# Two graph-attention layers on one core: the probabilities turned on VectorE and through DRAM, and the context taken transposed on column halves of the array

## The reference

```python
def layer(x, adj, Wq, bq, Wk, bk, Wv, bv, Wf, bf):      # 6 heads of 64
    h = relu(layernorm(x))
    q, k, v = heads(h @ Wq + bq), heads(h @ Wk + bk), heads(h @ Wv + bv)
    scores = einsum('bhqd,bhkd->bhqk', q, k) / 8
    probs  = softmax(scores + where(adj, 0, -9e15))
    ctx    = merge(einsum('bhqk,bhkd->bhqd', probs, v))
    return x + ctx @ Wf + bf
x = layer(x, adj, *weights_of_layer_0)
x = layer(x, adj, *weights_of_layer_1)
```

## Time and profile before

| | |
|---|---|
| median of three runs | 2083.96 us (2080.9 to 3268.01) |
| the profiled execution | 2084.19 us, span of its instructions 2081.6 us |
| TensorE matmul, weight load | busy 2023.3 us (97%), 1220.2 us (59%) |
| VectorE | 1757.7 us (84%) |
| ScalarE | 1268.3 us (61%) |
| GpSimd | 1335.0 us (64%) |
| DMA | 264.90 MB, 127 GB/s over the span |
| granted TensorE clock, mean | 0.992 of 2.4 GHz |

### The profile page before, as it was taken

How to read it: one execution, slowest core, us unless ns; L and a number is a source line. 1 busy time by engine, 2 the same in 40 slices (tenths; PEclk the granted TensorE clock), 3 DMA queues, 4 the chain that set the end, 5 groups by cost and what they waited for, 6 DMA issues and landing times.

```text
span 2081.6 us, 62061 instructions
## 1 busy us (share of the span) xinstructions
PE 2023.3 (97%) x18838; PEld 1220.2 (59%) x18838; DVE 1757.7 (84%) x6080; ACT 1268.3 (61%) x2249; POOL 1335.0 (64%) x1808
## 2 busy tenths in 40 slices
PE   4999999999999999999999999999999999999997
PEld 1556566566566556656665666666666666666664
DVE  6888888888888788888887888888888888888875
ACT  3566666666666566666665666666666666666653
POOL 3566666666666666666665666666666666666652
PEclk8999999999999999999999999999999999999998
DMA  6344444444444444444444444444444444444433
GB/s 192 98 113 120 131 127 123 129 135 135 136 122 125 121 135 135 134 115 130 132 137 127 129 119 133 131 135 136 127 119 133 131 136 136 129 117 117 114 98 99
DMA packets 443711, 264.90 MB, mean 127 GB/s; under 512 B 341986, under 2 KB 443364, under 8 KB 443364
## 3 DMA queue, kind: packets, MB, share of 16 engines
q1 hardware_dynamic: 443364, 260.76, 45.1%
HBM read 134.75 MB, written 125.83 MB: 125 GB/s over the span
## 4 chain that ended last, share of the span: by engine, by line
PE 37%; issue 26%; POOL 25%; DMA 4%; DVE 3%; SPq 3%; ACT 1%; POOLq 1%; DVEq 0%; ACTq 0%
PE ps_proj L497 7%; PE ps_proj L499 7%; PE ps_proj L498 7%; POOL ct_lo L426 6%; POOL x_tile L422 5%; POOL ht_lo L438 5%; PE ps_pt L540 4%; POOL rstd L411 3%; PE ps_out L497 3%; PE ps_out L498 3%; PE ps_out L499 3%; DMA c_moved<-c_dram 3%; PE ps_scores L573 3%; POOL probs L431 2%; SPq L338 2%
## 5 line engine op out<-in xcount | busy, mean ns | idle before, releaser
L431 POOL TENSOR_TENSOR probs<-probs,row_max 128x768 f32<-128x768 f32 x256 | 376.0, 1469 | 583.6 <-DVE row_max L878 583.6
L682 ACT ACTIVATE probs<-probs,exp_scale 128x768 f32<-128x768 f32 x256 | 239.7, 936 | 255.4 <-POOL probs L431 255.4
L856 DVE SCALAR_TENSOR_TENSOR qk_lo<-ps_proj,qk_bias,qk_hi 128x512 f16<-128x512 f32 x384 | 282.4, 737 | 129.2 <-ACT qk_hi L669 129.2
L878 DVE CUSTOM_DVE_ANT_0 probs<-ps_scores,mask 128x128 f32<-128x128 f32 x1536 | 342.2, 285 | 0.5 <-PE ps_scores L573 0.4
L638 ACT ACTIVATE pt_hi<-ps_pt 128x384 f16<-128x384 f32 x512 | 223.1, 487 | 147.2 <-PE ps_pt L540 146.6
L669 ACT ACTIVATE qk_hi<-ps_proj,qk_bias 128x512 f16<-128x512 f32 x384 | 258.9, 674 | 29.1 <-PE ps_proj L499 29.1
L841 DVE TENSOR_TENSOR pt_lo<-ps_pt,pt_hi 128x384 f16<-128x384 f32 x512 | 260.4, 550 | 2.4 <-ACT pt_hi L638 2.4
L497 PE MATMUL ps_proj<-wv_hi,ht_hi 128*128 128x384 f16 x768 | 251.7, 328 | 10.5 <-issue 5.4
L426 POOL TENSOR_TENSOR ct_lo<-c_moved,ct_hi 128x384 f16<-128x384 f32 x256 | 234.2, 915 | 36.3 <-ACT ct_hi L677 36.2
L422 POOL TENSOR_TENSOR x_tile<-x_tile,out_bias 128x384 f32<-128x384 f32 x256 | 256.2, 1001 | 0.5
L662 ACT ACTIVATE v_hi<-ps_proj 128x384 f16<-128x384 f32 x256 | 125.1, 489 | 211.9 <-PE ps_proj L499 211.8
(11 more groups left out here) (104 smaller groups left out, 5032.3 us busy)
## 6 DMA issues: line engine op xcount, KB each, us to landing
h_dram<-h_blocks SPq DMA_DIRECT2D x256, 192.0 KB, 1.9
h_moved<-h_dram SPq DMA_DIRECT2D x1024, 48.0 KB, 2.0
c_dram<-c_blocks SPq DMA_DIRECT2D x256, 192.0 KB, 1.9
c_moved<-c_dram SPq DMA_DIRECT2D x1024, 48.0 KB, 2.0
x_tile<-in_x SPq DMA_DIRECT2D x32, 768.0 KB, 5.0
out_x<-x_tile SPq DMA_DIRECT2D x128, 192.0 KB, 1.9
adj_u<-in_adj SPq DMA_DIRECT2D x64, 64.0 KB, 2.1
wv_raw<-in_L_gnn_Wv SPq DMA_DIRECT2D x2, 576.0 KB, 5.6
```

What stands on the lines that cost most here:

```text
L431: nc.gpsimd.tensor_tensor(probs[i % 2][:, :, :], probs[i % 2][:, :, :], row_max[i % 2][:, :].rearrange("p (a o) -> p a o", o=1) .to_broadc ...
L856: nc.vector.scalar_tensor_tensor(out=qk_lo[b][:, chunk, :], in0=ps_proj[bank_of("qk", chunk)][:, :], scalar=qk_bias[layer_of(t)][:, chunk ...
L878: ins = nc.vector.tensor_tensor_reduce(probs[i % 2][:, s, :], ps_scores[s // PAIRS][:, (s % PAIRS) * P:(s % PAIRS + 1) * P], mask[b][:, i, ...
```

## The change

- `turn_probs`, the halves of the probabilities (`probs_hi`, `probs_lo`), `normalise`, `ctx_turn` and the context's way through DRAM go.
- The exponential becomes six ACTIVATEs, one for each head, with the negated and scaled maximum as bias (`negate_max` on GpSimd) and the row sum as accumulator output. VectorE inverts the sums (`invert_sums`), and GpSimd scales the probabilities in fp32 (`scale_probs`).
- VectorE turns the 32x32 blocks of the probabilities (`probs_turn`, 768 columns), SP keeps them and brings them back, 384 KB each way.
- `apply_probs` runs three steps after the scores (two before). It makes the context transposed, in fp32: V (64 columns of a head) is the weight, the turned probabilities are the moving operand, even heads write the upper and odd heads the lower 64 partitions of `ps_ctx`.
- `ctx_hi` reads `ps_ctx` on ScalarE, `ctx_lo` moves from GpSimd to VectorE. V is copied in fp32 by VectorE alone (`v_out`), where it had a high and a low half.
- V has a bank of its own, Q and K have three, the context and the output one each.
- The order within a step changes on ScalarE (exponential of the graph before comes first) and on VectorE (turning the probabilities comes first).

```diff
             def slot(t, m):
                 for i in range(PER):
-                    cu, ci = graph_at(t, i, -3)
+                    pu, pi = graph_at(t, i, -2)
                     hu, hi = graph_at(t, i, 9)
                     su, si = graph_at(t, i, -5)
-                    if exists(cu):
-                        keep_blocks(cu, ci, c_blocked, c_blocks, c_dram, c_kept, c_back, m)
+                    if exists(pu):
...
                     if i == 3 and exists(t + 4) and layer_of(t + 4) == 0:
                         load_x(t + 4, m)
-                    if exists(cu):
-                        bring_back(cu, ci, c_dram, c_moved, c_kept, c_back, ct_set, m)
+                    if exists(pu):
+                        bring_back(pu, pi, p_dram, p_moved, p_kept, p_back, ctx_summed, m)
...
-            def subtract_max(t, i, m):
-                pool.wait_ge(masked, unit_count(t, m, PER, i + 1))
+            def negate_max(t, i, m):
+                wait_apart(pool, count, exp_done, unit_count(t, m, PER, i - 1))
+                wait_apart(pool, count, masked, unit_count(t, m, PER, i + 1))
+                nc.gpsimd.tensor_scalar(exp_bias[i % 2][:, :], row_max[i % 2][:, :], exp_scale[layer_of(t)][:, :],
+                                        -1.0, ALU.mult, ALU.mult).then_inc(bias_ready, 1)
+            def scale_probs(t, i, m):
+                pool.wait_ge(rcp_ready, unit_count(t, m, PER, i + 1))
                 nc.gpsimd.tensor_tensor(probs[i % 2][:, :, :], probs[i % 2][:, :, :],
-                                        row_max[i % 2][:, :].rearrange("p (a o) -> p a o", o=1)
-                                        .to_broadcast([P, HEADS, NODES]), ALU.subtract).then_inc(shifted, 1)
+                                        row_rcp[i % 2][:, :].rearrange("p (a o) -> p a o", o=1)
+                                        .to_broadcast([P, HEADS, NODES]), ALU.mult).then_inc(probs_ready, 1)
...
                         norm(nu, ni, m)
                     if exists(t + 1):
                         add_out_bias(t + 1, i, m)
-                    if exists(cu):
-                        ctx_lo(cu, ci, m)
+                    if exists(pu):
+                        scale_probs(pu, pi, m)
                     if exists(t):
-                        subtract_max(t, i, m)
+                        negate_max(t, i, m)
                     if exists(hu):
...
+            def apply_probs(t, i, m):
+                b = unit_no(t) % 2
...
-                if exists(ou) and ou < LAST - 2:
-                    pe.wait_ge(out_added, unit_count(ou, m, PER, oi + 1))
-                else:
-                    wait(pe, ctx_ready, unit_count(t, m, PER, i))
-                if (t, i) == (0, 0):
-                    pe.wait_ge(scales_set, LAYERS)
-                pe.wait_ge(pt_set, unit_count(t, m, 2 * PER, 2 * i + 2))
-                for s in range(HEADS):
-                    hd = head_of(s)
-                    mm = three(ps_out[:, hd * VW:(hd + 1) * VW], pt_hi[i % 2][:, s, :], pt_lo[i % 2][:, s, :],
-                               v_hi[b][:, i, hd, :], v_lo[b][:, i, hd, :])
+                wait(pe, ct_set, unit_count(t, m, PER, i))
+                pe.wait_ge(v_set, unit_count(t, m, PER, i + 1))
+                pe.wait_ge(p_back[i], unit_count(t, m, 16 * QUADS, 16 * QUADS))
+                turned = p_moved[i % 2][:, :, :].rearrange("p a (s k) -> p s a k", s=HEADS)
+                for c in range(PAIRS):
+                    for odd in range(2):
+                        hd = 2 * c + odd
+                        mm = pe.matmul(ps_ctx[odd * DH:(odd + 1) * DH, c * P:(c + 1) * P],
+                                       v[b][:, i, hd * DH:(hd + 1) * DH], turned[:, odd * PAIRS + c, :, :],
+                                       start=True, stop=True)
                 mm.then_inc(ctx_summed, 1)
...
                 l = layer_of(t)
                 if t < LAST - 2:
-                    cu, ci = graph_at(t, i, 2)
-                    pe.wait_ge(ctx_ready, unit_count(cu, m, PER, ci + 1))
+                    wait(pe, out_added, unit_count(t, m, PER, i))
                 else:
                     wait(pe, out_added, unit_count(t, m, PER, i - 1))
+                if (t, i) == (0, 0):
+                    pe.wait_ge(scales_set, LAYERS)
                 pe.wait_ge(ct_set, unit_count(t, m, PER, i + 1))
                 if unit_no(t) <= AHEAD and i == 0:
...
             def slot(t, m):
                 for i in range(PER):
-                    tu, ti = graph_at(t, i, -1)
-                    pu, pi = graph_at(t, i, -2)
+                    pu, pi = graph_at(t, i, -3)
                     ou, oi = graph_at(t, i, -4)
                     if exists(t + 1):
                         project_v(t + 1, i, m)
                     if exists(t):
                         score(t, i, m)
-                    if exists(tu):
-                        turn_probs(tu, ti, m)
                     if exists(pu):
                         apply_probs(pu, pi, m)
...
             def ctx_hi(t, i, m):
                 wait(act, out_summed, unit_count(t, m, PER, i - 1))
-                act.wait_ge(c_back[i], unit_count(t, m, 16 * QUADS, 16 * QUADS))
-                nc.scalar.activation(in_order(ct_hi[i % 2][:, :, :]), moved_in_order(c_moved[i % 2]), ACT.Copy
-                                     ).then_inc(ct_hi_set, 1)
+                act.wait_ge(ctx_summed, unit_count(t, m, PER, i + 1))
+                nc.scalar.activation(ct_hi[i % 2][:, :, :], ps_ctx[:, 0:H].rearrange("p (c k) -> p c k", c=KT),
+                                     ACT.Copy).then_inc(ct_hi_set, 1)
             def exp(t, i, m):
-                act.wait_ge(shifted, unit_count(t, m, PER, i + 1))
-                nc.scalar.activation(probs[i % 2][:, :, :], probs[i % 2][:, :, :], ACT.Exp,
-                                     scale=exp_scale[layer_of(t)][:, :]).then_inc(exp_done, 1)
+                wait(act, rcp_ready, unit_count(t, m, PER, i - 1))
+                act.wait_ge(bias_ready, unit_count(t, m, PER, i + 1))
+                for s in range(HEADS):
+                    ins = nc.scalar.activation(probs[i % 2][:, s, :], probs[i % 2][:, s, :], ACT.Exp,
+                                               bias=exp_bias[i % 2][:, s:s + 1], scale=exp_scale[layer_of(t)][:, :],
+                                               accum_out=row_sum[i % 2][:, s:s + 1])
+                ins.then_inc(exp_done, 1)
...
             def slot(t, m):
                 for i in range(PER):
-                    cu, ci = graph_at(t, i, -4)
+                    cu, ci = graph_at(t, i, -3)
                     nu, ni = graph_at(t, i, 10)
                     pu, pi = graph_at(t, i, -1)
                     hu, hi = graph_at(t, i, 8)
+                    if exists(pu):
+                        exp(pu, pi, m)
+                    if t == 1:
+                        weights_hi(1, CAST_ORDER[i])
                     if exists(cu):
                         ctx_hi(cu, ci, m)
+                    if exists(t + 1):
+                        for chunk in chunks_done(i, 0):
+                            qk_hi_out(t + 1, chunk, m)
                     if exists(nu):
                         relu(nu, ni, m)
-                    if t == 1:
-                        weights_hi(1, CAST_ORDER[i])
-                    if exists(t + 1):
-                        v_hi_out(t + 1, i, m)
-                    if exists(pu):
-                        probs_hi(pu, pi, m)
                     if exists(hu):
                         h_hi(hu, hi, m)
                     if exists(t + 1):
-                        for chunk in chunks_done(i, 0):
-                            qk_hi_out(t + 1, chunk, m)
                         if i == 2:
                             make_mask(t + 1, m)
-                    if exists(t):
-                        exp(t, i, m)
-                    if exists(t + 1):
                         for chunk in chunks_done(i, 1):
                             qk_hi_out(t + 1, chunk, m)
...
-            def turn_blocks(out, view):
-                return nc.vector.transpose(out.rearrange("p b (c k) -> p b c k", c=KT),
-                                           view.rearrange("p (c b r) -> p b c r", c=KT, b=QUADS))
+            def turn_blocks(out, view, cols):
+                return nc.vector.transpose(out.rearrange("p b (c k) -> p b c k", c=cols),
+                                           view.rearrange("p (c b r) -> p b c r", c=cols, b=QUADS))
...
-            def ctx_turn(t, i, m):
+                turn_blocks(h_blocks[i % 2][:, :, :], h[i % 2][:, :], KT).then_inc(h_blocked, 1)
+            def probs_turn(t, i, m):
                 du, di = graph_at(t, i, -2)
                 if exists(du):
-                    wait_apart(dve, count, c_kept[di], unit_count(du, m, 16, 16))
-                wait_apart(dve, count, ctx_ready, unit_count(t, m, PER, i + 1))
```

(68 more changed lines are left out.)

136 lines of the change are left out of this document (40 added, 96 removed).

## The result

The changed kernel takes 1997.11 us (median of four runs, 1990.15 to 1998.75), the kernel before, run on the same chip, 2082.85: a ratio of 0.9585 [0.9555, 0.9615], in which the one run of the kernel before that took 3268.01 us is left out. The forecast was 2008 us. The profiled execution took 1998.75 us with a span of 1996.6, which is 85.0 us less than the span in the earlier trace rows.

The account below looks back on a forecast made before the run. TensorE was taken as the bound, at 7.84 us a step: 2081.6 - 100 (shorter steps) + 19 (waits behind x's loads) + 5 (last steps) = 2006, given as 2008 us. Its own range was 1980 to 2045, the overall range 1972 to 2150.

Parts of the forecast that it names:

- TensorE's block: TensorE's context matmuls replacing transposes and context: 0.85 us (bound 1.38) against 1.25 removed, step 7.44 us, 100 us saved.
- rival 3: TensorE's context matmuls: weight loads exposed on column halves add 1.1 us, 9.1 us a step, 2400 us; chance 0.04.
- ScalarE: ScalarE's load: six exponentials with row sum at 0.55 us each, 3.3 a graph, 6.0 us a step, under 7.44.
- VectorE: VectorE's busy time: 694 us go and 542 come, leaving 1605 us, 6.3 us a step, under 7.44.
- rival 2: SP's transfer queue becomes the bound once stored probabilities take over 3.4 us to land; 2140 us, far end 2400; chance 0.12.
- The path from end to end: Probabilities' round trip, from V projection's start: fetches issued by 5.2 us, landed by 7.5 to 8, wanted by TensorE at 9.6.
- Waits behind x's load: TensorE waits for the probabilities' fetch when a 768 KB load of x goes ahead: 32 x 0.6 = 19 us.
- The end: The last eight steps hang on the longer exponential ring: 5 us added.
- The ring of exponentials: Exponentials, reciprocal, next graph's mask and maximum, negation, exponentials again: 5.6 us, binding only from an exponential block of 5.1 us.

## Why the prediction was right, step by step

**TensorE's block** was the term that decided, forecast at 0.85 us and measured at 0.81. That neighbouring passes on different halves run together is shown from three sides: 0.81 us alternating, 1.08 grouped, 1.45 on one half. The overlap is not the one I described, though. I let only the second pass of one matmul run beside the first pass of the next, 7 slots of 0.107 us and 0.10 for the change of shape. The records start in couples, which makes 6 slots of 0.109, with 0.05 more in the first and 0.10 more behind the last: a stronger overlap at nearly the same price. (The price of a pass also stood in the earlier trace rows, which the prediction overlooked: the six transposes are fp32 over 128 columns, 0.109 us apart.) The step came out at 7.52 us, of which 0.12 are fetch waits (29.0 us over some 245 steps); the forecast had 7.44 and, for the waits, 0.08 more. So the steady part lost 80.2 us where 100 less 19 were forecast; that these agree is luck, since the block gave 10 us more and the waits took 10 more.

**Weight loads** (rival 3). Each of the 3072 passes has its own (ns, min/median/max):

```profile
L521 PEld LDWEIGHTS ps_ctx<-p_moved,v x3072: 132/137/232, 83.5 to 1990.1; 128*64 128x64 f32 x192
```

Twelve of 0.137 us are 1.64 us; exposed, they alone would take twice the block's 0.81. The Trainium skill ("TensorE: Matmul & The Clock Gate", Part 3: Packing small matmuls) says that a load overlaps a running matmul only where the row group differs, which would expose them here, since column halves share every row; the trace disagrees, and the measurement decides. The same section's account of the mechanism also lets a load pass a running matmul when it goes to the background weight buffer; the hidden loads fit that, though no row names the buffer. The Trainium skill's 2.38 there for three column tiles, from which I had estimated 1.6 for two, stands beside 1.45/0.81 = 1.8.

**ScalarE.** Forecast 0.55 us an exponential and 3.3 a block; measured 0.475 from start to start and 2.85. The readout of the sum does have a row on this engine, 0.19 us, but half of it lies beside the end of its own exponential and half beside the start of the next. So the step was 5.6 us, not 6.0.

**VectorE.** 1586.8 us busy against 1605: the transpose took 0.968 us against 1.0.

**SP's queue** (rival 2). The slack was right, 0.43 against 0.4, out of two errors that cancelled: 384 KB landed in 2.4 us where I drew 2.9 between two sizes, and the rest of the step is 4.7 to 4.95 us (7.1 or 7.35 less 2.4), not 4.1: the stores and loads that I let lie within the wait stick out by 0.66 us in the steps that have both, and the four fetches of the probabilities took 2.00 us to issue on average, not 1.76. And it lay in every second step only. The path from end to end came out close: counted from the start of a V projection, its fetches were issued by 5.8 us (forecast 5.2), landed by 8.3 (7.5 to 8) and were used at 9.9 (9.6). This rival was nearer than its slack looked: a third of a microsecond more a step costs 53 us.

**Waits behind x's load.** The mechanism was right and the size was not: 28 waits for 40.6 us (21 for 29.0 in the steady part) where I had 32 of 0.6, 19 us. The last fetch landed 4.5 us after its issue there, inside my 4 to 5. But its issue ended at 5.6 us where I had 5.2, and without a wait TensorE reaches the context at 9.2 us where I had 9.6, since the load falls ahead of the shorter kind of step. The DMA share was 61.2%, the forecast some 65.

**The end.** The one term with the wrong sign: I added 5 us for the last steps, and the last stretch was 5.1 us shorter. Seven shorter steps are 2.2 of it; the cause of the other 3 stays open. The ring of exponentials does count there, as I had said: the stretch is 59.3 us long in the changed kernel, 67.5 with three further exponentials and 74.6 with five. Something outweighs it that I did not have. This 10 us and the block's 10 (0.04 x 250) against 10 to 20 more of fetch waits is how 2008 became 1997.

## What to carry to other kernels

Read what would hide an edit's cost from the order of issue, not from sums of busy time: six small matmuls were worth 0.44 us a step only because neighbours in the program lay on different halves of the array. Before a queue is trusted with a longer round trip, compute its slack step by step and not as a mean: 0.43 us on average was none in every second step and did not carry one more issue of 0.34. Cutting the rare large transfers into equal parts, one a step, took 29 us off here. An empty wait between a store and its fetch is not free time when what is put into it delays the fetch by more than the path's own room, which is another number than the queue's slack (1.5 us and 0.43 here).

## What the runs showed that I had not expected

- Grouped by half, the twelve passes took 1.08 us and not the 1.45 of one half. Sampled start by start, passes begin at 1018.06, .22, .33, .44, .55, .66, and a second series at .34, .50, .61, .71, .82, .93. The rows do not name the half; read as two halves, the second's first pass began before the first's were issued out, which program order alone would not give.
- A fp32 pass of 128 columns starts 0.109 us after its neighbour on the same half, in all three orders; only the second pass of each half comes later, 0.16 us after the first.
- Accumulating the row sum on ScalarE costs little: 128x128 exponentials with it are 0.48 us apart, though the two rows add up to 0.67.
- The same 768 KB cost differently by place: 40.6 us of TensorE's waits ahead of the fetch, 70.6 behind both fetches, 20.6 in quarters.
- SP issued a graph's four fetches of the probabilities in 1.75 us mostly, but in 2.30 at 1014.31 and 2.71 at 1029.69. Between 100 and 1900 us it took over 2 us in 68 of 239 steps, of which 64 were of one kind, every second step. I have no cause for it.
